# Writes of the split weights: sub 0 from SyncE's queue, sub 1 from ScalarE's

## The reference, cut to what matters

```
def cell(h, x):
    gi = x @ W_ih + b_ih
    gh = h @ W_hh + b_hh
    i_r, i_z, i_n = jnp.split(gi, 3, axis=-1)
    h_r, h_z, h_n = jnp.split(gh, 3, axis=-1)
    r = jax.nn.sigmoid(i_r + h_r)
    z = jax.nn.sigmoid(i_z + h_z)
    n = jnp.tanh(i_n + r * h_n)
    return (1.0 - z) * n + z * h
...
x = x + ffn(scan(cell, cond_2048, x), w_gate, w_up, w_down, ...)   # ffn rounds to FP8
```

## Time and profile before

| | value |
|---|---|
| median of three runs | 5935.98 us |
| the profiled execution | 5935.94 us |
| its span, first to last instruction | 5934.1 us |
| granted TensorE clock, mean share of full speed | 0.952 |
| busy: PE, DVE, ACT, POOL | 5107.1, 2915.2, 1824.6, 1739.0 us |
| DMA queue q1 (all transfers begun by SP) | 333.29 MB |
| first issue of line 202 to the landing of the last | 61.1 to about 248.6 us |

### The profile page before, as it was taken

One profiled execution on the slowest core, in us unless ns is written; L12 is line 12 of the kernel. 1 busy time (PEld: TensorE's weight loads), 2 busy tenths in 40 slices (PEclk: granted clock), 3 DMA queues, 4 the chain that ended last, 5 costly groups with the idle time before them and its releaser, 6 DMA issues. The chain is left out here.

```text
span 5934.1 us, 232765 instructions
## 1 busy us (share of the span) xinstructions
PE 5107.1 (86%) x102020; PEld 3343.8 (56%) x102020; DVE 2915.2 (49%) x5649; ACT 1824.6 (31%) x4050; POOL 1739.0 (29%) x801
## 2 busy tenths in 40 slices
PE   0299999999999999999999999999960599996665
PEld 0177766666666666666666667777650244442222
DVE  5244434447763444544464446426538311128887
ACT  4022222222222223522262226425502311114443
POOL 0133323333332331233213330441241000006776
PEclk9999999999999999999999999999985799998777
DMA  4411111111111111311131113544533100000111
GB/s 110 95 48 46 49 37 49 46 45 48 47 50 37 47 48 51 93 49 46 44 104 46 49 44 97 142 118 119 143 81 115 33 24 22 24 18 21 28 28 34
DMA packets 262286, 352.18 MB, mean 59 GB/s; under 512 B 47134, under 2 KB 214343, under 8 KB 261257
## 3 DMA queue, kind: packets, MB, share of 16 engines
q1 hardware_dynamic: 259689, 333.29, 20.4%
q0 software_dynamic: 1760, 5.77, 0.3%
HBM read 303.19 MB, written 28.33 MB: 56 GB/s over the span
## 5 line engine op out<-in xcount | busy, mean ns | idle before, releaser
L628 PE MATMUL psum<-whole_w,whole_hot 128*32 128x384 f16 x49152 | 3005.6, 327 | 27.0 <-issue 27.0
L635 PE MATMUL psum<-low_w,low_hot 128*32 128x384 f16 x24576 | 2100.2, 327 | 0.0
L628 PEld LDWEIGHTS psum<-whole_w,whole_hot 128*32 128x32 f16 x49152 | 1379.6, 97 | 653.8 <-issue 30.4
L577 ACT ACTIVATE whole_w<-run_high 32x384 f16<-32x384 f32 x1488 | 777.3, 522 | 2204.0 <-DVE run_high L784 2191.1
L522 POOL TENSOR_TENSOR whole_hot<-whole_a,whole_mask 48x2048 f16<-48x2048 f16 x192 | 692.8, 3609 | 2197.2 <-PE psum L628 1666.3
L784 DVE TENSOR_SCALAR run_high<-psum 128x384 int32<-128x384 int32 x372 | 207.6, 558 | 1593.7 <-PE psum L628 1500.3
L635 PEld LDWEIGHTS psum<-low_w,low_hot 128*32 128x32 f16 x24576 | 689.6, 97 | 312.1 <-issue 0.7
L674 PE MATMUL psum<-low_w,low_hot 64*64 64x384 f16 x20480 | 845.2, 323 | 21.3 <-DMA low_w<-w_rows 13.7
L791 DVE TENSOR_SCALAR whole_w<-psum 32x384 f16<-32x384 f32 x1488 | 821.9, 552 | 27.8
L674 PEld LDWEIGHTS psum<-low_w,low_hot 64*64 64x64 f16 x20480 | 635.0, 107 | 231.1 <-DMA low_w<-w_rows 36.1
L592 ACT ACTIVATE low_hot<-low_a,sum_scale 128x128 f16 x1536 | 469.8, 388 | 304.6 <-PE psum L674 267.1
(11 more groups left out here) (269 smaller groups left out, 3619.9 us busy)
## 6 DMA issues: line engine op xcount, KB each, us to landing
low_w<-w_rows SPq DMA_DIRECT2D x640, 144.0 KB
whole_w<-w_rows SPq DMA_DIRECT2D x768, 72.0 KB
low_w<-w_rows SPq DMA_DIRECT2D x384, 120.0 KB
low_w<-w_rows SPq DMA_DIRECT2D x640, 48.0 KB
low_w<-w_rows SPq DMA_DIRECT2D x384, 72.0 KB
w_rows<-w_split SPq DMA_DIRECT2D x128, 144.0 KB
work<-in_x SPq DMA_DIRECT2D x64, 128.0 KB, 2.6
out_y<-work SPq DMA_DIRECT2D x64, 128.0 KB, 2.3
```

The costliest lines, as they stand in the source:

```text
L577: last = nc.scalar.activation(whole_w[0:Q, buf, u * 2 + half, bq, :], run_high[own, u, :], ACT.Copy, scale=1.0 / HIGH_ONE)
L628: last = nc.tensor.matmul(run[m][u][j * Q:(j + 1) * Q, :], whole_hot[:, buf, sign, kk, j % 2 * Q:(j % 2 + 1) * Q], whole_w[:, buf, u * 2 + ...
L635: nc.tensor.matmul(run[m][u][j * Q:(j + 1) * Q, :], low_hot[:, buf, kk, j % 2 * Q:(j % 2 + 1) * Q], low_w[:, buf, cols(j // 2, u)], start= ...
```

## The change

The body of SP's loop moves into a helper that takes the engine, the chunk and the half. SP calls it for half 0 of each group q and ACT for half 1. The transfers themselves, 128 in all, their shapes, sources and targets are the same. The wait of DVE, and SP's last wait, count the same total. ACT's wait for its own `w3_ok` is now there for all eight chunks, and after `scale_rows(n + 2)` ACT waits for `split_ok` and then begins its eight transfers of chunk n.

```
+                    def write_rows(eng, n, sub):
+
+                        for q in range(PB):
+                            at = q * BK + sub * SK
+                            eng.dma_start(w_rows[n * PB + q, sub * W_KINDS * SK:(sub + 1) * W_KINDS * SK, :].rearrange("(j k) n -> k j n", j=W_KINDS),
+                                          split[at:at + SK, n % 2, :, :]).then_inc(moved[n % 2], 16)
+
                     @block.sync
...
                             sp.wait_ge(split_ok, n + 1)
                             sp.wait_ge(w3_ok, n + 1)
-                            for q in range(PB):
-                                for sub in range(SUBS):
-                                    at = q * BK + sub * SK
-                                    sp.dma_start(w_rows[n * PB + q, sub * W_KINDS * SK:(sub + 1) * W_KINDS * SK, :].rearrange("(j k) n -> k j n", j=W_KINDS),
-                                                 split[at:at + SK, n % 2, :, :]).then_inc(moved[n % 2], 16)
+                            write_rows(sp, n, 0)
...
                             nc.scalar.activation(split[:, n % 2, W3, :], rest[:, n % 2, :], ACT.Copy).then_inc(w3_ok, 1)
+                            a.wait_ge(w3_ok, n + 1)
                             if n + 2 < CHUNKS:
-                                a.wait_ge(w3_ok, n + 1)
                                 scale_rows(n + 2)
+                            a.wait_ge(split_ok, n + 1)
+                            write_rows(a, n, 1)
```

## The result

| | before | after |
|---|---|---|
| median | 5935.56 us (four runs) | 5870.68 us (four runs, 5864.17 to 5877.17) |
| ratio after / before, with 95% interval | | 0.9891 (0.9874 to 0.9908) |
| span of the profiled execution | 5934.1 us | 5875.4 us |
| writes of w_rows: mean rate, 61 to 183 us | 101 GB/s | 155 GB/s |
| the block behind the setup begins | 248.88 us | 183.10 us |

The kernel became 64.9 us faster, 1.1%. The forecast was 5928.1 us with a range down to 5895 us, and no clear change as the likeliest outcome: it was wrong, and the time lies outside its range.

The account below looks back on a forecast made before the run. The setup's writes were taken as bound by DMA engines sharing small stripes of partitions, not by issuing. SP 0, ACT 0, DVE 0 and transfers -7.8 us, from 5935.94, gave 5928.1 us, range 5895 to 5953 us.

Parts of the forecast that it names:

- no clear change: Whole kernel: a time within 0.2% of before, about 12 us; chance 0.51.
- What bounds the stage: Setup's writes of w_rows, 187.5 us: paced by DMA engines sharing a small stripe of partitions, with SP's issuing hidden.
- SP's and ACT's time: Issues taken from SP and added to ACT: 0 us each, with 3.5 us as cost if the cover fails.
- the cover: Between chunks: 3.7 us of data still queued after the last issue hide ACT's W3 and the restart of writes.
- The share of 0.45 to 0.50: Write stage: the busy share of the 16 DMA engines should stay at 0.45 to 0.50.
- The two queues' effect on the transfers: Write stage: rate rises to 105 GB/s through more regular mixing, 179.7 us against 187.5, a gain of 7.8 us.
- the bounds of 49 and 208 GB/s: Write stage: at worst all engines in step, 49 GB/s, 198 us slower; at best eight engines at 26 GB/s each.
- The second rival: Write stage: two queues spread engines over more stripes, 115 to 150 GB/s, 42 us less, 5894 us; chance 0.22.
- its sign of being wrong: Write stage: rate leaving 99 to 112 GB/s at the same share would mean mixing better or worse than assumed.
- nothing changes: Write stage: rate stays at 99 to 102 GB/s however packets are ordered, 5936 us give or take 3; chance 0.20.
- DVE's wait: DVE's waits for landings of w_rows should stay near 77 - 8 us.
- The medians of the issues: Issues inside write_rows: medians near 2.7 us on SP and ACT, twice 1386 ns, each queue draining at half pace.

Follow-up runs that it names:

- one_alt3: Against the kernel before: SP alone, each write cut in two of three kinds, order alternating between the halves; 5930.58 us beside 5930.12.
- two_same: Against the kernel before: each write cut in two, SP writing kinds 0-2 and ACT kinds 3-5 of the same eight partitions; 5944.87 us beside 5936.42.
- act_only: Against the kernel before: ACT begins all 128 writes in the same order, SP none; 5934.30 us beside 5936.42.
- same32: Against the changed kernel: SP takes both halves of q = 0, 1, 4, 5, ACT those of the others, 32 partitions apart; 5882.68 us.
- one_order64: Against the kernel before: SP alone, whole writes reordered so each is followed by the one 64 partitions further on; 5942.89 us beside 5941.44.
- two_half3: Against the changed kernel: SP on half 0, ACT on half 1, each write cut in two of three kinds; 5903.08 us, before 5936.42.
- wide16: Against the kernel before: SP alone writes each chunk in 6 transfers of 128 partitions, not 16 of 8; 5838.78 us, ratio 0.9835.
- one_half3: Against the kernel before: SP alone, each write cut in two of three kinds, order unchanged; 5986.27 us beside 5930.12.

## Why the prediction was wrong

**What bounds the stage: right.** The writes paced it, issuing was hidden, and the gain in the stage reached the end. one_alt3 shows that it was not the time of issuing: SP alone began 256 pieces in 171.5 us, at 0.67 us each. two_same has two issuers and no gain over before. act_only by itself decides nothing here, since a slow issue could be as slow on ACT.

**SP's and ACT's time: right in size.** The sum had 0 us for what now stands behind ACT's issues, and 3.5 us if the cover failed. act_only, the harder case with all 128 issues on ACT, cost 2.8 us; what it cost in the changed kernel itself was not measured apart.

**The share of 0.45 to 0.50: right,** at 0.49; ACT's writes use no other engines.

**The two queues' effect on the transfers: this step failed.** What rations the engines was named rightly, that many of them draw on one stripe at a time, and the bounds of 49 and 208 GB/s held. But within them I took 105 GB/s, on the ground that "two equal stripes under eight engines is what the drift gives already". The runs show that this does not hold. What drift gives depends on how often the stripe changes (84 against 110 GB/s in one queue) and, as far as the runs can tell, on how much is held (84 against 102 for pieces and whole writes). The change adds to both: 223 packets held in place of 98, and two stripes at a time. The rate was 155. 18.87 MB at 155 GB/s are 122 us; the term was 65.8 us and not 7.8.

**The evidence that misled.** The second rival was the right one. It had a chance of 0.22, priced at 115 to 150 GB/s, 42 us; even that was too low for the 155 GB/s and 65 us that came. The prediction had named a rate over 112 GB/s at the same share as its sign of being wrong, "mixing better" than assumed, and that is what came. Against this rival, and for "nothing changes", I held that the steady rate of one queue never leaves 99 to 105 GB/s "though the queue is always full". This is no evidence. A queue that holds about two writes is itself a limit on how far engines drift apart, and the change moved that limit. A steady rate under an unchanged limit says nothing on what happens when the limit goes. The rise from 49 to 112 GB/s, as soon as the engines stood over more than one write, was the reading to go by. The forecast counted it, and then took the row of today. The prediction also held its 99 to 105 GB/s beside a measured 104 and found agreement in size. That was chance: the same writes moved 155 GB/s.

**Two issuers on the same engines.** The Trainium skill, "DMA: Bandwidth & Descriptors", section "Issuing engines are not separate DMA queues", says that issuing from several engines saves only the sequencer's time. Here it does not hold: the time hidden on the sequencer was worth nothing, and the second queue gained 53% in rate on the same engines. In what it says of the engines it agrees with the trace: the share stayed at 0.49, so they are the same ones.

**DVE's wait** was put at 69 us and is 28.2: the same step, since it ends with the landings. The medians of the issues, put at 2.7 us, are 1.69 and 1.66 for the same reason.

**The 7 us that the profiled span lacks.** From the first matmul of the summing steps (line 674, 679 in after) to the first of the next stage (1522, 1527) it takes 2317.8 us before (2355.4 to 4673.2) and 2325.0 after (2289.6 to 4614.6). Over the profiles of the twelve kernels this stretch lies between 2313.6 us (same32) and 2327.4 (one_order64), without relation to the setup: act_only 2315.6, two_half3 2318.8, wide16 2324.1, one_half3 2325.8. The 13.8 us between them are nearly the spread of the nine runs of before (17.5 us). What in those steps varies stays open.

**What stays open.** How the gain of the whole change divides between more held and two stripes was measured with half-sized pieces only (84 to 100 to 124 GB/s); no run has two queues with whole writes on one stripe. That packets slow one another, and do so less in the faster versions, is seen in their durations. That engines get ahead of one another within what the queue holds fits all runs, but the trace does not tell which engine a packet ran on, so this is inferred and not seen.

## What to carry to other kernels

When the DMA engines are busy but move far less each than elsewhere in the trace, look at which partitions they stand on at the same time, and at the durations of packets of one size. Here transfers of eight partitions used half of the engines (share 0.49) and made them wait for one another. Better than a second queue was here a shape that spreads them, six transfers of 128 partitions in place of sixteen of eight (98 us against 65). And if a resource is steady under a full queue, ask what the size of the queue itself is worth before taking the steady rate for its limit.

## What the runs showed that was not expected

- A second issuing queue raised the rate of the same eight DMA engines from 101 to 155 GB/s at a busy share of 0.47 and 0.48.
- Cutting each write in two in one queue lowered the rate from 102 to 84 GB/s, with SP's issues still waiting for room (median 910 ns, minimum 277).
- The commonest duration of a packet of 3072 bytes was 121 ns before and after. At most 135 ns took 34% of them before and 79% after; in the first burst all took about four times as long (median 473 ns).
- The order of equal writes in one queue was worth 72 to 76 against 103 to 105 GB/s, depending on whether neighbours lie 32 or 64 partitions apart.
